# Attention scores of a gated cross-attention block: three bfloat16 parts on 48 and 112 rows, or two float32r parts on 48 rows

## The reference

```python
def xattn(x1, x2, Wq, bq, Wk, bk, Wv, bv):          # x1, x2: (B=32, C=128, L=512); 8 heads of 16
    q, k, v = proj(x1^T, Wq, bq), proj(x2^T, Wk, bk), proj(x2^T, Wv, bv)      # (B, 8, 512, 16)
    attn = softmax(einsum('bhqd,bhkd->bhqk', q, k) / sqrt(16))
    return einsum('bhqk,bhkd->bhqd', attn, v)       # back to (B, C, L)
x = x + tanh(g_xattn) * xattn(layernorm(x), ctx, ...)
x = x + tanh(g_ffn) * ffn(layernorm(x), ...)        # rmsnorm, router over 8 experts, top 2, plus a shared expert
```

## Time and profile before

| | |
|---|---|
| median of three runs | 1385.36 us |
| profiled execution, its own time | 1374.19 us |
| its span | 1372.4 us |
| granted TensorE clock, mean | 0.978 |
| TensorE / VectorE / ScalarE / GpSimd busy | 1279.6 / 922.4 / 880.6 / 813.8 us |
| TensorE weight loads busy | 658.0 us |

### The profile page before, as it was taken

The page is one execution under the profiler, slowest core; times in us unless marked ns, Lnnn a source line. Parts: engine busy times, 40 slices in busy tenths (PEclk is TensorE's granted clock), DMA queues, the critical chain, the costliest instruction groups (busy, mean ns, idle before and its releaser), DMA issues.

```text
span 1372.4 us, 33656 instructions
## 1 busy us (share of the span) xinstructions
PE 1279.6 (93%) x12198; PEld 658.0 (48%) x12198; DVE 922.4 (67%) x1307; ACT 880.6 (64%) x1778; POOL 813.8 (59%) x1014
## 2 busy tenths in 40 slices
PE   4899999999999999999898889999899999999997
PEld 1233332233322333333232223677688888888886
DVE  6999888889888889988787676467444333333332
ACT  2688888888888888888787778342324333333332
POOL 8665775776766767778786553104515555455553
PEclk7899999999999999999999999999999999999999
DMA  6545554555556456458665532537756898776665
GB/s 165 165 130 173 181 148 147 177 146 178 150 153 189 131 153 189 138 150 176 135 140 120 147 96 83 192 116 152 97 178 113 217 220 199 174 184 108 110 112 79
DMA packets 152542, 206.29 MB, mean 150 GB/s; under 512 B 33125, under 2 KB 82924, under 8 KB 152382
## 3 DMA queue, kind: packets, MB, share of 16 engines
q1 hardware_dynamic: 134126, 166.75, 44.1%
q0 software_dynamic: 18256, 37.38, 15.0%
HBM read 82.34 MB, written 61.94 MB: 105 GB/s over the span
## 4 chain that ended last, share of the span: by engine, by line
PE 23%; POOL 22%; SPq 21%; issue 14%; DMA 12%; DVE 3%; ACT 2%; POOLq 1%; ACTq 0%; DVEq 0%
PE m_banks L949 14%; SPq L450 11%; DMA arena<-rden_d 7%; SPq L446 4%; POOL map_d L725 3%; POOL arena L664 2%; POOL arena L661 2%; POOL arena L672 2%; POOL xs L674 2%; POOL xs L773 2%; PE bank L906 2%; POOL arena L662 2%; SPq L457 2%; SPq L464 2%; DVE row_max L1106 2%
## 5 line engine op out<-in xcount | busy, mean ns | idle before, releaser
L1106 DVE TENSOR_REDUCE row_max<-m_banks 128x2 f32<-128x1024 f32 x512 | 607.8, 1215 | 103.6 <-PE m_banks L854 102.5
L1386 ACT ACTIVATE arena<-bank 128x512 f32<-128x512 f32 x1024 | 551.1, 606 | 70.8 <-PE bank L875 69.5
L875 PE MATMUL bank<-arena 112*32 112x512 bf16 x4096 | 330.2, 386 | 30.8 <-DMA arena<-arena 22.5
L906 PE MATMUL bank<-arena 128*32 128x512 f32 x2048 | 273.3, 604 | 1.1 <-ACT arena L1400 0.5
L875 PEld LDWEIGHTS bank<-arena 112*32 112x32 bf16 x4096 | 102.4, 95 | 315.0 <-ACT arena L1386 153.8
L785 POOL DMA_INDIRECT out<-xs,arena x71 | 112.6, 1585 | 160.1 <-ACT xs L1478 123.8
L949 PE MATMUL m_banks<-w_ring,h_hi 128*128 x568 | 183.0, 403 | 0.0
L854 PE MATMUL m_banks<-arena 48*128 48x512 bf16 x1024 | 170.6, 394 | 12.6 <-DVE row_max L1106 12.0
L1467 ACT ACTIVATE arena<-m_banks 128x256 f32<-128x256 f32 x103 | 39.5, 384 | 185.8 <-PE m_banks L949 185.7
L672 POOL TENSOR_TENSOR arena<-arena 128x512 f32<-128x512 f32 x32 | 41.0, 1282 | 173.5 <-DMA arena<-rden_d 169.4
L949 PE MATMUL m_banks<-w_ring,h_lo 128*128 x284 | 111.7, 393 | 0.0
(11 more groups left out here) (185 smaller groups left out, 1893.6 us busy)
## 6 DMA issues: line engine op xcount, KB each, us to landing
arena<-arena SPq DMA_DIRECT2D x256, 128.0 KB
arena<-arena SPq DMA_DIRECT2D x384, 64.0 KB
split_d<-staged SPq DMA_DIRECT2D x30, 512.0 KB, 5.3
w_ring<-split_d SPq DMA_DIRECT2D x60, 256.0 KB, 4.1
arena<-in_w SPq DMA_DIRECT2D x36, 256.0 KB, 5.9
arena<-in_ctx SPq DMA_DIRECT2D x32, 256.0 KB, 3.8
xs<-in_x SPq DMA_DIRECT2D x32, 256.0 KB, 4.2
arena<-rden_d SPq DMA_DIRECT2D x32, 256.0 KB
```

What stands on the lines that cost most here:

```text
L875: last = nc.tensor.matmul(out[c, :], k_stack[b % 3][0:SHIFTED, h, kt * P + c.start:kt * P + c.stop], q_stack[b % 3][0:SHIFTED, h, :], star ...
L906: last = nc.tensor.matmul(pv_ps[2 * DH * j:2 * DH * (j + 1), :], v_ones[b % 3][:, kt, GROUP * g + j, :], probs[pair % 3][:, j, :], start=( ...
L1106: nc.vector.reduce_max(pair, m_ps[(STEPS * b + u) // 2 % M_PAIRS], AX_X).then_inc(s_mx, 1)
L1386: nc.scalar.activation(probs[group % 3][:, j, :], bank_of["scores", b, s], ACT.Exp, scale=float(DH) ** -0.5).then_inc(s_exp, 1)
```

## The change

Scores are computed from two float32r parts (high and low) of k and q. A head has one group of 48 rows: high.high, high.low, low.high; even heads lie at partitions 0 to 47, odd heads at 64 to 111, so the stacks are 4 pairs wide and as large as before. Row 48 (and 112) holds the negated maximum in `q_stack` and 1.0 in `k_stack`. Maxima use 48 rows as before; the exponential's scores are one matmul of 49 rows and 128 weight columns a head, on the lower or the upper half of the array. Also:

- The high part is made by POOL instead of ACT; `split` is a copy and one subtraction, `rest` and the middle part are gone. 12 DMAs of 128 KB replace 18 of 128 or 64 KB a batch.
- `maxima_parts` is gone; `turn_maxima` is a float32 matmul of the maxima themselves, and ACT negates them.
- On TensorE the side products stand behind `values`; `EVAC_AT`, `take_turned`, `take_logits` are two steps later, `STAGE_AT` two earlier.
- At the start, `ident_b` and the fills of `q_stack`'s middle rows are gone; `k_stack` is filled with 1.0 as a whole.

```diff
-SLOTS_OF = (((HI, HI), (HI, MID), (MID, LO)), ((HI, LO), (MID, MID), (HI, HI)))
-COPIES = tuple(sum(2 if first == second else 4 for first, second in slots) for slots in SLOTS_OF)
+SLOTS_OF = ((HI, HI, LOW), (HI, LOW, HI))
+COPIES = 2 * len(SLOTS_OF[0])
-EVAC_AT = {25: (3, 0), 29: (3, 1), 9: (2, 2)}
-HIGH_AT = (27, 31)
-PARTS_AT = (15, 31)
+EVAC_AT = {27: (3, 0), 31: (3, 1), 11: (2, 2)}
-STAGE_AT = 15
+STAGE_AT = 13
...
+                for at, slot in enumerate(SLOTS_OF[n]):
+                    if slot == part:
+                        for a in range(2):
+                            rows = stack[LANE * a + at:LANE * a + at + STACK - 2:len(SLOTS_OF[n]), :, :]
+                            sp.dma_start(rows.bitcast(F32), src[a:P:2, :].bitcast(F32)).then_inc(s_cp[n], DMA)
...
             for i in TURNS:
                 if is_b(i + 2):
                     copy_parts(i + 2, 0, HI)
-                    copy_parts(i + 2, 0, MID)
...
-                    copy_parts(i + 2, 0, LO)
+                    copy_parts(i + 2, 0, LOW)
...
-                    copy_parts(i + 2, 1, MID)
-                    copy_parts(i + 2, 1, LO)
+                    copy_parts(i + 2, 1, LOW)
...
             def split(b, n):
+                pool.wait_ge(s_evac, 3 * b + n + 1)
+                pool.wait_ge(s_part, 2 * b + n)
+                pool.wait_ge(s_cp[n], COPIES * DMA * b)
+                hi, lo = parts[n]
+                nc.gpsimd.tensor_copy(hi, proj[n]).then_inc(s_hi, 1)
                 pool.wait_ge(s_hi, 2 * b + n + 1)
-                nc.gpsimd.tensor_tensor(mid, proj[n], hi, ALU.subtract).then_inc(s_part, 1)
-                link(nc.gpsimd.tensor_tensor(rest, proj[n], hi, ALU.subtract))
-                nc.gpsimd.tensor_tensor(lo, rest, mid, ALU.subtract).then_inc(s_part, 1)
+                nc.gpsimd.tensor_tensor(lo, proj[n], hi.bitcast(F32), ALU.subtract).then_inc(s_part, 1)
...
-                    rows, h = slice(LANE * a, LANE * a + STACK), GROUP * g + 2 * j + a
+                    rows, h = slice(LANE * a, LANE * a + STACK), GROUP // 2 * g + j
...
-                nc.tensor.matmul(out[0:2 * GROUP * KT, 0:P], m_parts[half][:], ident_b[:],
+                nc.tensor.matmul(out[half_rows[half], 0:P], row_max[b % 2][:, n * half:n * (half + 1)], ident[:],
                                  start=True, stop=True).then_inc(s_mt, 1)
...
-                for c in COLUMNS:
-                    last = nc.tensor.matmul(out[c, :], k_stack[b % 3][0:SHIFTED, h, kt * P + c.start:kt * P + c.stop],
-                                            q_stack[b % 3][0:SHIFTED, h, :], start=True, stop=True)
-                last.then_inc(s_es, 1)
+                nc.tensor.matmul(out, k_stack[b % 3][rows, h, kt * P:(kt + 1) * P], q_stack[b % 3][rows, h, :],
+                                 start=True, stop=True).then_inc(s_es, 1)
...
-                    if s == TURN_TOKENS_AT and is_b(i - 3):
-                        turn_tokens(i - 3)
-                    if s == LOGITS_AT and is_b(i - 3):
-                        router_logits(i - 3)
-                    if s in PROJECT_AT and is_b(i + PROJECT_AT[s][0]):
-                        project(i + PROJECT_AT[s][0], PROJECT_AT[s][1])
                     if is_b(i):
                         exp_scores(i, s + 2)
                         exp_scores(i, s + 3)
...
                         values(i, s // GROUP - 1)
+                    if s == TURN_TOKENS_AT and is_b(i - 3):
+                        turn_tokens(i - 3)
+                    if s == LOGITS_AT and is_b(i - 3):
+                        router_logits(i - 3)
+                    if s in PROJECT_AT and is_b(i + PROJECT_AT[s][0]):
+                        project(i + PROJECT_AT[s][0], PROJECT_AT[s][1])
```

More of the change, by code:

```diff
@@ L133, in build @@
             staged_both = under("staged", [P, 2, L])
+        with ExitStack() as tiles:
+            q_stack = [tiles.enter_context(nc.sbuf_tensor(f"q_stack{i}", [P, HEADS // 2, L], F32R)) for i in range(3)]
+            tiles.enter_context(nc.sbuf_tensor("below_k", [P, 3, GROUP, L], F32))
+            k_stack = [tiles.enter_context(nc.sbuf_tensor(f"k_stack{i}", [P, HEADS // 2, L], F32R)) for i in range(3)]
         staged = [staged_both[:, part, :] for part in range(2)]
@@ L143, in build @@
         proj = [a.take(L) for _ in range(2)]
-        rest = a.take(L)
-        held = [a.take(3 * L // 2, BF16).rearrange("p (t l) -> p t l", t=3) for _ in range(2)]
-        parts = [[held[n][:, part, :] for part in (HI, MID, LO)] for n in range(2)]
+        parts = [[a.take(L, F32R) for part in (HI, LOW)] for n in range(2)]
         wq, wk, wv = (a.take(P) for _ in range(3))
-        m_rows = [a.take(P // 2, BF16)[0:2 * GROUP * KT, :] for _ in range(2)]
+        rows_both = a.take(P, F32R)
+        half_rows = [slice(2 * DH * half, 2 * DH * half + GROUP * KT) for half in range(2)]
+        m_rows = [rows_both[half_rows[half], :] for half in range(2)]
         attention_end = a.at
@@ L205, in build @@
         row_max = [sb(f"row_max{i}", [P, HEADS * KT]) for i in range(2)]
-        m_parts = [sb(f"m_parts{i}", [P, 2 * GROUP * KT], BF16) for i in range(2)]
-        ident_b = sb("ident_b", [P, P], BF16)
         mv2 = sb("mv2", [P, B, 2])
@@ L1392, in take_maxima @@
                     act_e.wait_ge(s_row[half], DMA * b)
-                nc.scalar.copy(m_rows[half], bank_of["maxima", b, half][0:2 * GROUP * KT, 0:P]).then_inc(s_mr, 1)
+                nc.scalar.activation(m_rows[half], bank_of["maxima", b, half][half_rows[half], 0:P], ACT.Copy,
+                                     scale=-1.0).then_inc(s_mr, 1)
             def take_values(b, g):
@@ L1440, in _ @@
                         staged_high(i + 2)
[L1441 removed]
+                    if s == TURN_TOKENS_AT + 3 and is_b(i - 3):
                         take_turned(i - 3)
```

102 lines of the change are left out of this document (30 added, 72 removed).

## The result

The changed kernel takes 1387.52 us (median of 20 runs, 1379.02 to 1393.98) against 1381.58 for the kernel before (20 runs on the same chip, 1366.68 to 1392.35): ratio 1.0045, 95% interval 1.0027 to 1.0063. The change costs half a per cent or nothing; 6% less was forecast.

A forecast was written before the change was run, and what follows sets the result against it. The loop of SP and POOL (24.26 us a round), TensorE right below, was taken to bound the kernel; 59.3 us from 23 turns, 20 from five late ones and 4.5 at the ends made 83.8 less: 1302 us, range 1262 to 1365.

The forecast's parts named there:

- GpSimd's high copy: POOL's copy making the high part in `split`, no row in the profile: 0.77 us taken, between nothing and 1.58.
- the 0.66 of the sum: SP's time per DMA issue in its loop with POOL: 0.66 us each, 18 issues instead of 20, 11.9 us.
- The loop of SP and POOL: Reciprocals' transfer, `add_attention`, `split` and SP's DMA issues, one round a turn: 24.26 us, to become 20.3.
- The five late turns: Turns in which the routing's scatters fall: 28.67 us each, to become 24.7, 4.0 less each.
- VectorE's and ScalarE's work: Their work a turn after `maxima_parts` and two casts go: 20.6 us for VectorE, 20.5 for ScalarE.
- the open question: Whether float32r score matmuls overlap on the array's halves: TensorE 19.8 us a turn if so, 26.8 if not.
- Rival D: TensorE's clock drops as it is less busy: at 0.8 it needs 24.8 us, time about 1350 us; chance 0.06.
- The turn is the longest of loop 20.3, engines 22.4 and TensorE 19.8, plus 0.3 for their meeting: Attention loop's turn as its longest bound plus 0.3: 22.7 us instead of 25.28, 59.3 us less over 23 turns.
- My group of 1.96 us: TensorE's group of four steps without side product, halves overlapping: 0.22 + 0.44 + 0.22 + 0.86 + 0.22 us.
- The sign that I had named for being wrong: The prediction would be wrong if attention turns stayed above 24.5 us, or another DMA issue time made the loop bind.
- the 3.8 us of my sum: TensorE's side products and turning of maxima a turn: 24.14 - 20.3 = 3.8 us.
- the stall term: ScalarE and VectorE idle because side products moved behind the values: 1.8 us a turn for either, bounds 0 and 3.5.

The follow-up runs named there:

- e4: Changed kernel with all score matmuls on the lower half of the array, odd heads' scores left out; ratio 1.1093 to the kernel before.
- e9: Changed kernel with ScalarE's exponentials over 256 of 512 columns, half of them left out; ratio 0.9775 to the kernel before.
- e8: Changed kernel with parts, stacks and maxima rows in bfloat16 instead of float32r, losing score precision; ratio 0.9847 to the kernel before.
- e12: Kernel before without copies of the low parts from the fourth batch on, 16 DMAs a turn instead of 20; ratio 0.9963 to the kernel before.
- e1: Changed kernel with its side products back between the maxima and the third exponential tile; ratio 0.9976 to the kernel before.
- e13: Changed kernel again, unaltered, as a control on another chip; ratio 1.0003 to the kernel before.
- e15: Kernel before with each projection cut into two halves of 256 columns, between maxima and third tile; ratio 1.0032 to the kernel before.

## Why the prediction was wrong

**Right.** GpSimd's high copy takes 0.61 us (0.77 predicted, bounds 0 and 1.58) and the low part 1.28; SP's copies still start 0.64 us apart with rows twice as long (0.64 and 0.65 before; the 0.66 of the sum is a mean over all 20). The loop of SP and POOL no longer binds: SP has 0% of the chain, and GpSimd waits, between 100 and 700 us, 34.9 us for ScalarE's projection before the high copy and 87.5 us for VectorE's statistics, beside 71.7 us for the reciprocals. The five late turns were predicted at 24.7 us and took 25.7. VectorE's and ScalarE's work came to 19.86 x 25.8 / 25 = 20.5 and 20.4 us a turn, predicted 20.6 and 20.5. The halves overlap for float32r (e4), which was the open question. The granted clock was 1.00, the level of 2.4 GHz, in both windows and in every ordinary turn; short stretches at 1.2 GHz fell in three turns from the nineteenth on (0.94, 0.87 and 0.94 in these turns). Rival D, with 0.8 throughout, did not occur.

**Wrong, and decisive: "The turn is the longest of loop 20.3, engines 22.4 and TensorE 19.8, plus 0.3 for their meeting".** None of the three is what came next. The step assumes that an engine's work can always be done while the others do theirs. A group is paced instead by a path through two engines in turn: first tile, its exponential, then either the fourth tile in the same bank and the values (2.61 us) or the copy of the earlier values and the values (2.75 us). My group of 1.96 us had no wait in it at all. The sign that I had named for being wrong, turns above 24.5 us, is what came: 25.8. e9 shortens only ScalarE's piece of the path, and the turn falls by 1.9 us although ScalarE had a fifth of its time free; e8 shortens only the tiles' piece, and the turn falls by 0.9. What stands behind the values comes on top of the path: the six groups with side products or turnings take together 3.8 us more than six of 2.75, and 22.0 + 3.8 = 25.8 us is the measured turn. That this equals the 3.8 us of my sum is chance: mine was 24.14 - 20.3, with the busy time of 25 us taken for that of a turn, and the same groups of e12 take 4.4 us more than six of 2.54.

The trace of before had the sign. Its pair of tiles ahead of the values takes 0.60 us in one group (370.12 to 370.72) and 0.44 in the one that has a side product between (373.68 to 374.12). I read the 0.44 and passed over the 0.60. The 0.16 us are no wait for a bank; they are the values' wait for ScalarE's copy of the earlier ones, L1400 there, which ends at 370.58:

```profile
369.50 0.60 ACT L1386 ACTIVATE arena<-bank 128x512 f32<-128x512 f32 x1 [0.45 <-PE bank L875]
370.00 0.58 ACT L1400 COPY arena<-bank 128x512 f32<-128x512 f32 x1
```

So the 2.54 us are the same path: first tile 0.46, exponential and copy 1.08, 0.14, values 0.86. The change shortens no piece of it and lengthens two, the first tile to 0.54 and the values, with the change of layout behind them, to 1.00: 2.75. It could not have brought such a group to 1.96.

**In the wrong sum: the stall term, "I take 1.8 us a turn for either".** I charged the moved products to ScalarE and VectorE as starvation, within their own sums of 20.5 us. Their move costs 0.9 us a turn (e1), less than I took, but it falls on the path itself, on top of 24.9.

**Mis-sized: TensorE's group of 1.96 us.** From the starts in the trace after, with the wait taken out, it is 0.34 + 0.47 + 0.43 + 1.00 = 2.24 us; the first pair shows 0.34 and not 0.22, since its load comes exposed behind the values (0.23 in e8). TensorE's turn is then 8 x 2.24 + 3.8 = 21.7 (an estimate), not 19.8. That alone would not have broken the forecast.

**The loop removed was worth little.** It was real (24.26 us, rightly summed), but e12 took 2.6 us from it and gained 0.4%. In the late turns TensorE did wait for the copies before, and the changed kernel saved 14.8 us there; I had said 20. I gave the change the whole distance from 25.28 to 22.7 us because the chain of waits ran through SP and POOL; a chain shows who came last, not by how much.

**Open.** Why e1's late turns stretch to 30 us and the changed kernel's do not. In each of e1's two longest, 29.1 and 30.8 us, 6.8 us ran at 1.2 GHz. In the second the clock fell behind a stop: TensorE, VectorE and ScalarE all stood for 3.4 to 3.9 us, up to 773.3, while GpSimd issued scatters (L709), and went on when VectorE's copy of the logits (L1071) ran. The same stop stands five times in e9's late turns (3.6 to 5.4 us); what released it, the traces don't show. So it isn't shown either that the changed kernel's even late turns come from the loop's removal alone. Also open: the 4.7 us behind the last turn, which may be scatter, as that stretch took 523.7 us in the trace before and 528.4 after, but 530.4 in e13, the same kernel, and 526.5 in e15, whose code there is that of before; what a fourth bank would bring where the maxima lose none; and what the copy of the values would cost in another place of ScalarE's order, which no run tried.

## What to carry to other kernels

Where one engine fills a ring of n buffers in program order and another empties it, follow buffer k to its user k + n through both engines, for every position in the group, and add everything that both do in between (here also the copy that frees the one bank of the values): that path is a lower bound of the turn beside the engines' sums, and it stays when the work shrinks. Before crediting a change with the removal of a loop, price the next path, and take the loop away alone in an experiment if it can be done. A filler put into such a wait gains only what it leaves over after its own changes of layout and the buffer it takes itself.

## What the runs showed of the hardware

- TensorE was "busy" 24.68 of 25 us and waited 0.4 to 0.5 us in each of the three groups shown all the same, since a record of 0.50 us can be followed by the next start after 0.34. The Trainium skill (Perfetto Trace Analysis, Identifying the Most-Contended Engine) says that the busy share of matmuls is no good measure of the distance to roofline, since they are pipelined; the trace agrees. Starts show what lengths hide.
- Four float32r matmuls of 48 rows and 512 columns, two on each half of the array, take 0.47 us from start to start with the next; on one half 0.91.
- A passage between 64-row halves and 32-column quarters costs about 0.1 us: 0.56 - 0.47 and 1.00 - 0.89 with float32r tiles, and 1.00 us from values to tiles with bfloat16 ones too.
- Values start 0.14 us after ScalarE's copy that frees their bank has ended, in the traces of before, after, e8, e9 and e12 alike.
- GpSimd casts 128 x 512 from float32 to float32r in 0.61 us, cheaper than its scaling of the same tile (0.77).
- VectorE reduces 128 x 512 from PSUM in 0.68 us and a pair, 128 x 1024, in 1.22: splitting the pair costs 0.15 us, 16 times a turn.
